# Layer 1's cross-attention: the output projection as three products of rounded weights and outcomes

## The reference, cut to what matters

```
x = x + xattn(layernorm(x), ctx, ctx, mask)
q = (query @ Wq.T + bq)       # 16 heads of 32, 512 tokens
k = (keys @ Wk.T + bk); v = (values @ Wv.T + bv)
energy = q k^T;  energy[mask == 0] = -1e20
out = softmax(energy / sqrt(32)) @ v          # back to (8, 64, 512)
return out @ Wo.T + bo
x = x + mlstm(layernorm(x), ...)              # what comes next
```

## Time and profile before

| what | value |
|---|---|
| median of three runs | 1667.64 us (1663.56 to 1668.69) |
| the profiled execution | 1670.61 us, its span 1668.8 us |
| TensorE busy | 1633.3 us, 98% of the span |
| VectorE busy | 1035.9 us, 62% |
| ScalarE busy | 822.6 us, 49% |
| TensorE in the chain that ended last | 90% |
| mean granted TensorE clock | 0.993 of full |

### The profile page before, as it was taken

How to read it: one execution, slowest core, us unless ns; L and a number is a source line. 1 busy time by engine, 2 the same in 40 slices (tenths; PEclk the granted TensorE clock), 3 DMA queues, 4 the chain that set the end, 5 groups by cost and what they waited for, 6 DMA issues and landing times.

```text
span 1668.8 us, 27415 instructions
## 1 busy us (share of the span) xinstructions
PE 1633.3 (98%) x10627; PEld 1301.1 (78%) x10627; DVE 1035.9 (62%) x2121; ACT 822.6 (49%) x1635; POOL 242.1 (15%) x321
## 2 busy tenths in 40 slices
PE   8999999999999999999999999999999999999997
PEld 6777777777777666577999986777767778899997
DVE  6334344444457786573666675767664876699996
ACT  5333333333334535552655564545545453487785
POOL 0100000000001401342111112311100304021111
PEclk9999999999999999999999999999999999999999
DMA  6111010100142004045999962111231053599994
GB/s 248 39 76 51 27 51 26 44 34 30 73 165 101 2 1 177 26 157 169 374 394 384 386 238 76 43 55 39 83 127 51 26 213 113 220 362 368 370 370 126
DMA packets 44783, 246.74 MB, mean 148 GB/s; under 512 B 5912, under 2 KB 6416, under 8 KB 21856
## 3 DMA queue, kind: packets, MB, share of 16 engines
q1 hardware_dynamic: 32368, 216.83, 34.3%
q0 software_dynamic: 7664, 19.68, 4.2%
q10 hardware_dynamic: 4608, 8.33, 1.3%
HBM read 229.21 MB, written 16.13 MB: 147 GB/s over the span
## 4 chain that ended last, share of the span: by engine, by line
PE 90%; DVE 5%; ACT 1%; issue 1%; POOL 1%; DMA 1%; SPq 0%; POOLq 0%; ACTq 0%; DVEq 0%
PE bank L723 29%; PE bank L290 9%; PE bank L2566 7%; PE bank L914 3%; PE bank L3739 3%; PE bank L942 3%; PE bank L296 3%; PE bank L3207 2%; PE bank L1642 2%; PE bank L853 2%; PE bank L2175 2%; PE bank L2177 2%; PE bank L2176 2%; PE bank L1699 2%; PE bank L1322 2%; PE bank L1613 1%
## 5 line engine op out<-in xcount | busy, mean ns | idle before, releaser
L723 PE MATMUL bank<-split 128*128 128x512 f32 x2160 | 521.2, 395 | 0.0
L723 PEld LDWEIGHTS bank<-split 128*128 128x128 f32 x2160 | 397.7, 188 | 90.3 <-issue 5.3
L922 ACT COPY normed<-bank 128x512 f32<-128x512 f32 x128 | 68.9, 591 | 121.3 <-PE bank L914 121.3
L885 DVE TENSOR_REDUCE small<-bank 128x1 f32<-128x512 f32 x64 | 43.9, 686 | 132.1 <-PE bank L853 132.1
L783 DVE COPY arena<-bank 128x512 f32<-128x512 f32 x76 | 52.5, 690 | 113.4 <-PE bank L723 113.4
L290 PEld LDWEIGHTS bank<-arena,weights 128*128 128x128 f32 x992 | 117.0, 194 | 5.1 <-issue 2.9
L290 PE MATMUL bank<-arena,weights 128*128 128x128 f32 x992 | 117.5, 277 | 2.5 <-issue 2.0
L2566 PE MATMUL bank<-up_high_r,tok_r 128*128 128x352 f32 x512 | 108.2, 323 | 0.0
L766 ACT COPY arena<-bank 128x512 f32<-128x512 f32 x76 | 44.5, 587 | 125.3 <-PE bank L723 102.9
L904 ACT ACTIVATE normed<-bank,small 128x512 f32<-128x512 f32 x64 | 44.1, 690 | 124.0 <-DVE small L887 123.7
L2566 PEld LDWEIGHTS bank<-up_high_r,tok_r 128*128 128x128 f32 x512 | 86.5, 188 | 0.0
(11 more groups left out here) (481 smaller groups left out, 3385.2 us busy)
## 6 DMA issues: line engine op xcount, KB each, us to landing
weights<-in_L_ffn_re_w SPq DMA_DIRECT2D x62, 1024.0 KB, 8.5
weights<-in_L_w SPq DMA_DIRECT2D x20, 1408.0 KB, 9.1
arena<-in_ctxT SPq DMA_DIRECT2D x23, 1024.0 KB, 4.9
arena<-in_L_w SPq DMA_DIRECT2D x12, 1408.0 KB, 8.5
weights<-in_L_w_full SPq DMA_DIRECT2D x10, 1280.0 KB, 10.4
weights<-in_L_ffn_sw SPq DMA_DIRECT2D x9, 1024.0 KB, 4.9
expert_out<-arena ACTq DMA_DIRECT2D x31, 256.0 KB, 8.3
arena<-in_L_w_full SPq DMA_DIRECT2D x6, 1280.0 KB, 11.0
```

The source lines that it names most:

```text
L723: s = pe.matmul(bank[:, :], still, moving, start=(n == 0), stop=(n == len(order) - 1))
L922: act.copy(self.probT[s], blocks(banks[5 + s][:, :], CTX // P)).then_inc(self.probT_a.sem, 1)
```

## The change

The weights of the output projection and the outcomes are split as well. In sequence 7's first unit (unit 28) ScalarE casts the four slices of `x1_o` into `keys1_r[0]` (a buffer of keys that are no longer read), and VectorE writes the rest in place over the weights. In unit 28 + u the outcomes of tile u are split, from `qT` into `outs1_high_r` (two buffers in turn, new) and `outs_r`. For tile 3 this is cut in two: the first three slices in unit 31, the fourth after the attention, on both engines. TensorE's `project` becomes twelve matmuls of rounded operands a tile.

```diff
@@ CrossAttention.__init__, the plan
+                if layer == 1 and c == self.steps - 1:
+                    splits += [("w", "o", 0, k) for k in range(KT)] if u == 0 else []
+                    splits += [("out", u, 0, KT - u // (NT - 1))]
...
+            else:
+                self.split_order.append(("out", NT - 1, KT - 1, KT))
@@ wait_split_source
+            elif s[0] == "out" and self.layer == 1:
+                e.wait_ge(self.out_v.sem, self.out_v.at(self.quads * (2 * s[1] + 2) - (1 if s[1:3] == (NT - 1, 0) else 0)))
+                if s[1] >= 2:
+                    e.wait_ge(out_mm, NT * 3 + s[1] - 1)
...
-                if s[1] == "o":
+                if s[1] == "o" and self.layer == 1:
+                    e.wait_ge(self.scored.sem, self.scored.at(self.quads * (self.steps - 1)))
+                elif s[1] == "o":
@@ cross1_scalar
         x1.attend_scalar(act)
+        x1.split_scalar(act, x1.split_order[-1])
@@ cross1_vector
         x1.attend_vector(dve, beside)
+        x1.split_vector(dve, x1.split_order[-1])
@@ cross1_tensor, project(i)
-            pe.wait_ge(x1.out_v.sem, x1.out_v.at(x1.quads * (2 * i + 2)))
-            output_tile(pe, x1.qT, ["x1_o"], i, banks[i % 3])
+            t, order = slice(i * P, (i + 1) * P), [(k, a, b) for k in range(KT) for a, b in ((0, 0), (0, 1), (1, 0))]
+            pe.wait_ge(x1.low.sem, x1.low.at(x1.split_no["out", i, 0, KT - i // (NT - 1)]))
+            for n, (k, a, b) in enumerate(order):
+                if i == NT - 1 and k == KT - 1 and a == b == 0:
+                    pe.wait_ge(x1.low.sem, x1.low.at(x1.split_no["out", i, k, KT]))
+                still = (outs1_high_r[:, i % 2 * KT + k, :], outs_r[:, k, t])[a]
+                moving = (keys1_r[0][:, k, :], weights["x1_o"].rounded[:, k, :])[b]
+                s = pe.matmul(banks[i % 3][:, :], still, moving, start=(n == 0), stop=(n == len(order) - 1))
+            s.then_inc(out_mm, 1)
```

More of the change, by code:

```diff
@@ L171, in build_program @@
     plain_r = {z: rounded("plain_" + z, NW * SLOT + at, SLOT)[:, :].rearrange("p (k n) -> p k n", k=KT) for z, at in PLAIN_AT.items()}
+    outs1_high_r = rounded("outs1_high_r", NW * SLOT + EXPERTS_END, 2 * DIM)[:, :].rearrange("p (k t) -> p k t", k=2 * KT)
     KEYS1_AT, QBLK_AT = (17280, 12288), 14592
@@ L678, in split_tensors @@
                 t = slice(s[1] * P, (s[1] + 1) * P)
+                if self.layer == 1:
+                    at = s[1] % 2 * KT
+                    return outs1_high_r[:, at + s[2]:at + s[3], :], outs_r[:, s[2]:s[3], t], self.qT[:, s[2]:s[3], t]
                 return outs_high_r[s[1] % 2][:, s[2]:s[3], :], outs_r[:, s[2]:s[3], t], self.qT[:, s[2]:s[3], t]
             w = weights[f"x{self.layer}_{s[1]}{s[2] if self.parts > 1 else ''}"]
+            if s[1] == "o" and self.layer == 1:
+                return keys1_r[0][:, s[3], :], w.rounded[:, s[3], :], w.view[:, s[3], :]
             if s[1] == "o":
```

## The result

| | before | after |
|---|---|---|
| median of 20 runs | 1665.96 us (1663.56 to 1669.44) | 1668.87 us (1667.71 to 1672.04) |
| ratio, 95% interval | | 1.0020 [1.0014, 1.0026] |
| profiled span | 1668.8 us | 1668.0 us |

The change made the kernel slower by 2.9 us, between 2.3 and 4.3 by the interval. That is inside what was called no change (5 us) and on the side of the forecast, which was +1.8 us. The forecast time was 1669.4 us, but that it lies only 0.5 us off is in part luck: it was counted from a median of three runs (1667.64 us), and over 20 runs the kernel before has 1665.96. The range, 1664.0 to 1673.5, holds the times of all rivals, so it decides nothing between them; the profile has to.

What follows compares the result with a forecast made beforehand. Taken as bound by TensorE up to unit 31's turns, then by ScalarE and VectorE. Terms -2.1, +1.3, +1.4, +0.7 gave +1.3 us on the profiled span; against the median +1.8 was taken: 1669.4 us, range 1664.0 to 1673.5.

Steps and rivals of the forecast that it cites:

- TensorE's part: Output tiles: 2.75 us each instead of 3.44; three stand in the chain, so TensorE could be 2.1 us earlier at unit 31.
- Unit 28: Five casts on ScalarE and five subtractions on VectorE fit into waits there: 0 to 0.3 us lost, taken as 0.
- VectorE becomes the bound of unit 31: Unit 31's softmax starts at 1242.0 instead of 1242.77, without a pause; only 0.8 of 2.1 us is left: +1.3 us.
- ScalarE's queue: Unit 31: copies end 1.3 us sooner, but the second cast ahead of the table load delays it 0.6 us: +1.4 us.
- The clock: Behind the fourth output tile: the clock falls before or during the first 16 narrow gate matmuls: +0.7 us.
- the gain survives: Rival: tile 1's statistics do not hold back the last outcome, the table load moves forward: -1.3, up to -3.0 us; chance 0.12.
- Slower through VectorE: Rival: unit 28's five subtractions end after 1229.73, the evacuation and all behind it slip: 0.9 to +4.2 us; chance 0.15.

Runs made afterwards that it cites:

- late_cast: The changed kernel with the last 128x128 cast moved behind the table load and two roots, its subtraction behind two normalised tiles: 1665.80 us, 0.9998 of the kernel before.
- products_small: The kernel before with twelve rounded matmuls a tile on small rests of the context, no casts or subtractions, projection left out: 1663.79 us, 0.9990 of before.

## Why the prediction was right, step by step

- **TensorE's part.** Right: 2.92 and 2.75 us where 3.61 and 3.44 stood.
- **Unit 28.** Right, with nothing to spare: the evacuation starts as the fifth subtraction ends. VectorE's last evacuation of values starts at 1226.64, 0.04 us behind the turns' place in the chain, exactly as before (1229.73 against 1229.69). ScalarE still waits 2.49 us behind its five casts.
- **VectorE becomes the bound of unit 31.** Right: its softmax starts at 1238.91, 12.31 behind the turns of unit 28 against 13.08 before; 0.8 us ahead, as worked out, with no pause in front of it.
- **ScalarE's queue.** Right in mechanism and size: the copies 1.3 us sooner, the table load 0.59 us later (0.6 forecast). late_cast shows that it is this cast: 1.9 us with the one move.
- **The clock.** Right in mechanism: it fell ahead of the third gate tile in all three profiled executions, and filling the gap brought it back. The prediction says that its trace fell "behind busy transposes"; just ahead of that fall stood twelve transposes and 21 of the narrow matmuls, as the profile counts them, and no run here tells which of the two let it fall. For the pair of profiles the size was right too: the last turn +1.34 us, +1.3 forecast. That it fits to 0.04 is luck: the last turns of one program lie up to 1.7 us apart, and other pairs of the six profiled executions give +0.2 to +3.3. The term that was too small is the last of the sum. The clock was put at +0.7 on the path; the averages of three give 1.0 (1.6 without the queue's 0.6). For the median I added 0.5 us because the profiled execution of before holds nearly the full price of the lower clock; by the medians it should have been 1.6 (2.9 - 1.3).
- **What stays open** is the other side of that term. The three profiled executions of each kernel give +1.6 us at the last turn, and behind it the two kernels run alike (90.9 to 91.4 us from the last turn in the timeline to the first wide products of the experts, in all six). The 20 runs give +2.3 to +4.3. The mean granted clock, which is on record for every timed run too, closes most of this. Over the 60 runs of before beside the experiments it is 0.9958, over the 20 of after 0.9943, and over the three profiled executions 0.9943 for either kernel. So the profiled executions of before had more of the lower clock than its timed runs mostly have. The difference of 0.0015 is 2.5 us of TensorE's time, at most, since a lower clock beside the path costs nothing; with the queue's 0.6 it makes 3.1 where the medians give 2.9. In which stretch the timed runs lost it is not on record.
- The rival "the gain survives" is nearest to late_cast and products_small: it needed the second cast out of ScalarE's way. In late_cast the third gate tile starts 1.1 us sooner than before, and the median gains 0.3. "Slower through VectorE" did not happen in unit 28; in unit 31 VectorE's subtraction is on the chain, as in the forecast.

## What to carry to other kernels

Before adding a short instruction to an in-order queue, look at what it waits for and not only at what it takes: a cast of 0.3 us cost 1.9 because its source comes behind another engine's queue, and a table load that needed nothing stood behind it. Where TensorE gains in front of a stretch that other engines set, the gain becomes idle time, and idle time in front of narrow matmuls can lower the clock for the wide ones that follow (here, in the averages of three, it fell 2.4 us sooner, and stayed at half for up to 10.2 us instead of 6.8). Count positions from an anchor just ahead of the change: the queues then repeat to 0.03 us, and what is left is the clock.

## What the runs showed of the hardware that I had not expected

The place where the granted clock falls differs by some microseconds between executions of one program, and the time at half clock by 3.4 us, with all queues alike to 0.03 us. In this kernel that is one part of the spread of 6 us between runs, and 1.7 and 1.4 us of it in this stretch alone (last turn at 33.02 to 34.71 before, 34.91 to 36.27 after). Over the whole program the clock and the time of a run go together: of 60 timed runs of before, the 20 with a mean granted clock of 0.997 took 1664.3 us on average and the 15 with 0.994 took 1667.7. Eighteen added wide matmuls made a program 3 us faster.
